# Node features for the messages kept as fp32 rows, spread by four fp32 matmuls in place of twelve bf16

## The reference, cut to what matters

```python
h = jnp.maximum(_layernorm(x, axis=-1), 0.0)
e = shifted_softplus(edge_attr_128 @ W1 + b1) @ W2 + b2      # per edge
x = x + jax.ops.segment_sum(h[dst] * e, src, num_segments=n)  # sender = dst, receiver = src
# second layer: a two-step relational graph convolution over gathered rows of h @ W[r]
```

## Time and profile before

| what | value |
|---|---|
| median of 3 runs | 7132.72 us (7132.13 to 7136.48) |
| profiled execution, its own time | 7149.41 us |
| its span | 7147.6 us |
| `prepare` | 0 to 154 us |
| `filter_layer` | 155 to 2712 us |
| `make_table` and `convolve` twice | 2712 us to the end |

### The profile page before, as it was taken

One profiled execution on the slowest core, in us unless ns is written; L12 is line 12 of the kernel. 1 busy time (PEld: TensorE's weight loads), 2 busy tenths in 40 slices (PEclk: granted clock), 3 DMA queues, 4 the chain that ended last, 5 costly groups with the idle time before them and its releaser, 6 DMA issues. The chain is left out here.

```text
span 7147.6 us, 113836 instructions
## 1 busy us (share of the span) xinstructions
PE 4359.0 (61%) x28573; PEld 3531.3 (49%) x28573; DVE 3819.8 (53%) x11981; ACT 2911.5 (41%) x7788; POOL 5383.4 (75%) x5304
## 2 busy tenths in 40 slices
PE   2888888888888887645555555555444444444444
PEld 1666666667777773444444444444333333333333
DVE  8888888868777877645555555555211111111111
ACT  2666666654444446523333333333222222222222
POOL 6777777778888885577777777777677777777777
PEclk6999999999999998756666666666555555555555
DMA  3766666589998988634444443333222222222222
GB/s 107 188 183 182 181 181 162 149 173 190 188 189 186 192 166 273 209 89 104 106 106 106 105 105 105 106 105 103 67 55 56 56 56 56 56 56 56 56 56 54
DMA packets 688258, 879.21 MB, mean 123 GB/s; under 512 B 132110, under 2 KB 512426, under 8 KB 687277
## 3 DMA queue, kind: packets, MB, share of 16 engines
q1 hardware_dynamic: 446088, 530.23, 26.9%
q0 software_dynamic: 238864, 340.26, 21.9%
q10 hardware_dynamic: 2634, 1.21, 0.1%
HBM read 615.41 MB, written 255.76 MB: 122 GB/s over the span
## 5 line engine op out<-in xcount | busy, mean ns | idle before, releaser
L1907 POOL DMA_INDIRECT got<-table_dram,cidx x3322 | 3154.0, 949 | 1057.3 <-issue 996.9
L1956 PE MATMUL bank<-got,share 128*128 128x128 f32 x6656 | 1632.7, 422 | 1856.0 <-DMA got<-table_dram,cidx 1855.5
L1956 PEld LDWEIGHTS bank<-got,share 128*128 128x128 f32 x6656 | 1400.6, 311 | 2010.3 <-DMA got<-table_dram,cidx 2009.7
L1536 POOL DMA_INDIRECT msg_dram<-total,idx x1008 | 986.7, 979 | 335.3 <-issue 281.1
L2010 ACT ACTIVATE share<-cto_node,etcol 128x128 f32<-128x128 bf16 x3328 | 1071.1, 393 | 354.0 <-DVE cto_node L2101 318.4
L1551 POOL DMA_INDIRECT acc_dram<-total,idx x653 | 1035.7, 1586 | 206.5 <-issue 194.6
L2000 ACT ACTIVATE cidx<-srccol 128x4 int32<-128x4 f32 x832 | 169.5, 205 | 2395.2 <-PE bank L1956 2381.6
L303 DVE SCALAR_TENSOR_TENSOR xs<-bank,mask_hi,xs 128x128 f32 x416 | 146.2, 351 | 1690.0 <-PE bank L1956 1690.0
L1129 PEld LDWEIGHTS bank<-w,soft 128*128 128x128 f32 x3328 | 446.1, 195 | 56.7 <-issue 41.5
L1129 PE MATMUL bank<-w,soft 128*128 128x128 f32 x3328 | 447.1, 278 | 0.0
L1120 PE MATMUL bank<-edges_t,w 128*128 128x512 f32 x832 | 428.9, 597 | 2.4 <-DVE soft L1360 2.4
(11 more groups left out here) (262 smaller groups left out, 7877.8 us busy)
## 6 DMA issues: line engine op xcount, KB each, us to landing
edges<-in_edge_attr SPq DMA_DIRECT2D x415, 256.0 KB
unit<-msg_dram SPq DMA_DIRECT2D x616, 129.0 KB
clow<-rows_dram SPq DMA_DIRECT2D x416, 128.0 KB
got<-table_dram,cidx POOLq DMA_INDIRECT x3322
table_dram<-made SPq DMA_DIRECT2D x98, 512.0 KB, 5.0
table_dram<-umade SPq DMA_DIRECT2D x98, 512.0 KB, 3.0
low<-rows_dram SPq DMA_DIRECT2D x164, 256.0 KB
win<-split_dram SPq DMA_DIRECT2D x416, 96.0 KB
```

The lines of the kernel that those rows point to most:

```text
L1536: pool.indirect_dma_start(g.msg_dram[:, :], bass.IndirectOffsetOnAxis(ap=idx[k][:, j:j + 1], axis=0), total[k][:, j, :], None).then_inc(s_ ...
L1907: pool.indirect_dma_start(got[k][:, j, :], None, g.table_dram[which][:, :], bass.IndirectOffsetOnAxis(ap=idx[k][:, j:j + 1], axis=0)).then ...
L1956: ins = nc.tensor.matmul(window[k], share[k][:, j, :], got[ka][:, j, :], start=j == 0, stop=j == TG - 1)
```

## The change

- `split_dram` (three bf16 parts, 768 bytes a row) becomes `feat_dram` (fp32, 512 bytes a row). Stores and window loads shrink from 96 KB to 64 KB for 128 rows.
- The splitting is gone: in `prepare` 22 casts on ACT and 22 subtractions on DVE, in the filter stage 44 of each. SP's stores wait for ACT alone.
- `h` in `prepare` has 6 buffers, and ACT waits for the store of the chunk six before.
- `to_edge` is fp32 in the order (part, edge), and DVE's comparison that makes it reads `low` with a step of 4 elements.
- `spread` runs one fp32 matmul for each of the four parts, not three bf16 ones.

Of the diff, in this order: DVE's list in `prepare`, SP's store, ACT's chunks, two tiles of the filter stage, PE's `spread`, DVE's `edge_hot`, DVE's plain steps.

```diff
-            split_chunks(0, 2)
             moments(1)
-            split_chunks(2, 3)
             variance(1)
-            split_chunks(3, 4)
             constants()
...
             def store(c):
-                k = c % NSP
-                sp.wait_ge(s_part3, c + 1)
-                sp.dma_start(g.split_dram[c * CB * P:(c + 1) * CB * P, :].rearrange("(b p) f -> p b f", p=P),
-                             split[k][:, :, :, :].rearrange("p b k f -> p b (k f)")).then_inc(s_split_out[k], 16)
+                k = c % NH
+                sp.wait_ge(s_h, c * CB + CB)
+                sp.dma_start(g.feat_dram[c * CB * P:(c + 1) * CB * P, :].rearrange("(b p) f -> p b f", p=P),
+                             h[k][:, :, :]).then_inc(s_h_out[k], 16)
...
-            def split_chunk(c):
+            def feature_chunk(c):
-                need(act, s_rest1, c - NH + 1)
+                need(act, s_h_out[c % NH], c // NH * 16)
                 for i in range(c * CB, c * CB + CB):
                     nc.scalar.activation(h[c % NH][:, i - c * CB, :], g.xs[:, i, :], ACT.Relu,
                                          bias=g.shift[:, i:i + 1], scale=g.rstd[:, i:i + 1]).then_inc(s_h, 1)
-                act.wait_ge(s_h, c * CB + CB)
-                need(act, s_split_out[c % NSP], c // NSP * 16)
-                nc.scalar.activation(split[c % NSP][:, :, 0, :], h[c % NH][:, :, :], ACT.Copy).then_inc(s_part1, 1)
-                if c >= LAG:
-                    second_part(c - LAG)
...
-        win = [sb(f"win{k}", [P, 3 * F], BF16) for k in range(NE)]
+        win = [sb(f"win{k}", [P, F]) for k in range(NE)]
-        to_edge = [sb(f"to_edge{k}", [P, P, TG], BF16) for k in range(2)]
+        to_edge = [sb(f"to_edge{k}", [P, TG, P]) for k in range(2)]
...
                     for j in range(TG):
-                        for part in range(3):
-                            ins = nc.tensor.matmul(bank[:, j * F:(j + 1) * F], to_edge[k][:, :, j],
-                                                   win[s.slot(NE, 2)][:, part * F:(part + 1) * F],
-                                                   start=windows.own and part == 0, stop=part == 2 or not windows.own,
-                                                   skip_group_check=not windows.own)
+                        ins = nc.tensor.matmul(bank[:, j * F:(j + 1) * F], to_edge[k][:, j, :], win[s.slot(NE, 2)][:, :],
+                                               start=windows.own, stop=True, skip_group_check=not windows.own)
...
-                v.tensor_scalar(to_edge[k][:, :, :].rearrange("p a b -> p (a b)"), low[s.slot(NE, 2)][:, 0, :],
+                v.tensor_scalar(to_edge[k][:, :, :], low[s.slot(NE, 2)][:, 0, :].rearrange("q (p j) -> q j p", j=TG),
                                 g.want[:, bass.ds(s.at(2), 1)], None, ALU.is_equal).then_inc(s_hot, 1)
...
-                    if s.slot(CHUNK_STEPS, 0) == 1:
-                        chunk_remainder(s.use(CHUNK_STEPS, 0))
-                    if s.slot(CHUNK_STEPS, 0) == 3:
-                        chunk_third(s.use(CHUNK_STEPS, 0))
```

More of the change, by code:

```diff
@@ L326, in prepare @@
     NCH, NEARLY = g.NCH, g.NEARLY
-    NSP = 4
-    NH = 4
-    NR = 3
-    LAG = 2
+    NH = 6
     PART = NCH // 3
@@ L403, in prepare @@
         h = [sb(f"h{k}", [P, CB, F]) for k in range(NH)]
-        rest = [sb(f"rest{k}", [P, CB, F]) for k in range(NR)]
-        split = [sb(f"split{k}", [P, CB, 3, F], BF16) for k in range(NSP)]
         s_binned = sem("p_binned")
@@ L429, in prepare @@
         s_h = sem("p_h")
-        s_part1 = sem("p_part1")
-        s_rest1 = sem("p_rest1")
-        s_part2 = sem("p_part2")
-        s_part3 = sem("p_part3")
-        s_split_out = [sem(f"p_split_out{k}") for k in range(NSP)]
+        s_h_out = [sem(f"p_h_out{k}") for k in range(NH)]
         x_rest = N - (NBLK - 1) * P
@@ L476, in _ @@
             sp.wait_ge(s_rows, 12 * 16)
-            for k in range(NSP):
-                sp.wait_ge(s_split_out[k], 16 * len(range(k, NEARLY, NSP)))
+            for k in range(NH):
+                sp.wait_ge(s_h_out[k], 16 * len(range(k, NEARLY, NH)))
         @block.gpsimd
@@ L564, in _ @@
                     act.wait_ge(s_norm, 4)
-                split_chunk(c)
+                feature_chunk(c)
                 if c == PART - 3:
                     deviation(1)
-            for c in range(NEARLY - LAG, NEARLY):
-                second_part(c)
             columns(2)
@@ L1015, in load_window @@
                 first = sp.value_load(g.base[0:1, bass.ds(s.at(2), 1)], min_val=0, max_val=g.NROWS)
-                sp.dma_start(win[k][:, :], g.split_dram[bass.ds(first, P), :]).then_inc(s_win[k], 16)
+                sp.dma_start(win[k][:, :], g.feat_dram[bass.ds(first, P), :]).then_inc(s_win[k], 16)
             def clear(chunk, j):
@@ L1249, in copy_factor, with chunk @@
                 nc.scalar.activation(factor[s.slot(2, 2)][:, :], bank_e[:, :], ACT.Copy).then_inc(s_ec, 1)
-            def chunk_first(m):
+            def chunk(m):
                 for b in range(CB):
@@ L1321, in other_program @@
             def other_program():
-                chunk_first(0)
-                chunk_second(0)
+                chunk(0)
                 with act.Fori(1, g.NLATE) as m:
-                    chunk_first(m)
-                    chunk_second(m)
+                    chunk(m)
                 adding(Windows(g, False), 0, PEEL)
@@ L1514, in own_program @@
                 adding(Windows(g, True), NA, 16)
-            def other_program():
-                chunk_remainder(0)
-                chunk_third(0)
-                with dve.Fori(1, g.NLATE) as m:
-                    chunk_remainder(m)
-                    chunk_third(m)
-                adding(Windows(g, False), 0, PEEL)
-            if_own(dve, g, own_program, other_program)
+            if_own(dve, g, own_program, lambda: adding(Windows(g, False), 0, PEEL))
         @block.gpsimd
```

72 lines of the change are left out of this document (12 added, 60 removed).

## The result

| kernel | median | range, runs |
|---|---|---|
| before | 7135.67 us | 7129.54 to 7137.83, 8 |
| changed | 7153.89 us | 7149.21 to 7158.30, 8 |

The changed kernel is slower: ratio 1.0027, 95% interval 1.0017 to 1.0036, or 18.2 us. The forecast was 7120.5 us, 12.2 us faster than the 7132.72 known then. The profiled execution of the changed kernel takes 7153.8 us.

A forecast was written before the change was run, and what follows sets the result against it. POOL's transfers were taken to bound the filter stage and DVE's list prepare. Prepare -13.9, first filter group -0.3 and POOL's holding +2 gave -12.2 us, from 7132.7 to 7120.5 us; range 7108 to 7135 us for 8 in 10.

The forecast's parts named there:

- Prepare: Stage before the filter stage: without DVE's 22 subtractions it ends 13.9 us earlier, between 11.1 and 14.8.
- rival 4: In prepare, POOL gets no relief and stays the bound: 7123.3 us; 55% together with the forecast itself.
- gap ahead of the second third's moments: Sign in DVE's list in prepare: none expected; a gap there would be the nodes' load.
- PE's spread: Filter stage, PE: 0.22 us longer a group with fp32 products, hidden under POOL's time, 0 us.
- to_edge's length: Filter stage, DVE: the fp32 comparison takes 0.49 us, +0.13, hidden by 0.8 us to spare, 0 us.
- What POOL itself feels: Filter stage: POOL's transfers lengthen when they start inside to_edge, +2 us in sum, between -12 and +22.
- The price: Filter stage: each POOL transfer started inside to_edge takes 0.10 us longer, read from one held transfer.
- The count: Filter stage: POOL starts falling into to_edge go from 103 to 138 over plain and adding groups.
- The missing subtractions: Filter stage, late chunks: DVE's 44 subtractions fall away, which had caught 19 POOL starts, -1.9 us.
- Rival 2: Filter stage: POOL is held for all that is left of to_edge, +13 us, 7131.5 us in all; 20%.
- Rival 3: Filter stage: POOL and DVE fall into step, a start meeting to_edge in every group, 7208 us; 8%.

The follow-up runs named there:

- e1b: Kernel before with only to_edge made fp32, PE's products still bf16, at the upper clock: 7170.74 us against 7137.21, ratio 1.0047.
- e5: Changed kernel with 22 fp32 subtractions put back into DVE's list in prepare, low clock: 8335.05 us beside 8549.64 for the kernel before.
- e6: Changed kernel with to_edge back in bf16 and twelve bf16 products on the window's upper halves, low clock: 8530.73 us against 8549.64, ratio 0.9980.

## Why the prediction was wrong

- **Prepare: right.** Forecast -13.9 us, measured -12.3 at DVE's end (141.87 against 154.19) and -13.0 at the first transfer. POOL ended at 137.9 us, forecast 138.6, so rival 4 didn't come. DVE had no gap ahead of the second third's moments.
- **PE's spread: right.** 1.06 us in 8 records, hidden at the upper clock.
- **to_edge's length: right** (0.48 at best and 0.503 us on average, forecast 0.49), and hidden as length: POOL never waited longer than its 0.3 us.
- **"What POOL itself feels", +2 us: the step that failed.** It measured +29.3 us, over its own upper bound of +22. Three things in it were wrong.
  - The price. I took 0.10 us a start from the earlier trace rows and read it as a weak hold, because `to_edge` had 0.22 us to run. It was a full hold from the mark on, 0.12 us into the transfer: 0.22 - 0.12 = 0.10. That was the very same number under a rule that I didn't look for, and one row can't tell the two. By the rule, a longer `to_edge` raises the price of a hit, from 81 to 192 ns in the plain groups (2.8 us over 34, 14.6 over 76).
  - The count. I took every start inside `to_edge` for a hit, 72 and 31 before and 96 and 42 now. Held were 34 and 9 before and 76 and 32 now. The first 0.22 us of `to_edge` hold nobody, so the longer form doubled the part that does.
  - The others. I counted `to_edge` alone. By count `to_edge` cost 11.8 + 3.1 = 14.9 us more. `to_node`, which the change doesn't touch, cost 8.8 us more in the plain groups, where it held the successor of a transfer held by `to_edge` 65 times of 76; it was 1 of 34 before, when most of these transfers missed it by a few hundredths of a us. `unit_hot` cost 5.7 us more in the adding groups. The missing subtractions gave back 2.8 us, forecast 1.9. This sum is 26.6 us; `same<-low` and the one-hots add 2.5.
- **The rivals.** Rival 2 (held for all of `to_edge`, 20%) had the mechanism of a hit, but its +13 us left out the other instructions and counted the starts as I did. Rival 3 (falling into step, 8%) had the other half in a milder form, a third of the groups and not all. Each alone gave a wrong time. The Trainium skill, SBUF — State Buffer, section "Who interferes with whom", says of DVE's two-port modes that whoever issues first has the shared pair of ports for the whole instruction, and that the other is blocked. Taken at its word it gave +13 and was nearer than my row. The trace agrees with it once the wait is counted from 0.13 us after the start, for transfers whose mark comes 0.22 us or more into `to_edge`; it doesn't show which mode DVE was in.
- **Still open.** Why transfers met `unit_hot` 123 times after 96, though its place in DVE's order stands. It went with the fp32 form in e1b too (119); over all traces it is 89 to 102 times with a bf16 `to_edge` by DVE and 118 to 126 with an fp32 one in a single piece, and 117 and 110 with short pieces. Why the first 0.15 to 0.22 us of an instruction hold nobody is not shown either, only that it is so. The swaps' worth in time by themselves at the upper clock was not reached; only the combination was.

## What to carry to other kernels

Where POOL's indirect transfers are the bound, the DVE instructions that run beside them are part of the bound: ask of each how long it is (a hit waits to its end, and here its first 0.15 to 0.22 us hit nobody), whether all its inputs lie in SBUF, and what stands one transfer period behind its end. A longer instruction with the same work can cost more than its length times its hits, and cutting it into short pieces can pay though DVE gets busier, as it did for `to_edge` and `same<-low`, and not shown for `to_node`. One row of a held transfer doesn't give a price; plot the excess against what was left of the other instruction over some tens of rows before a step rests on it.

## What the runs showed of the hardware

- The hold is on tensor operations with two SBUF inputs, too. `to_node`, a comparison of two bf16 SBUF operands, held transfers for 0.16 us on average, in the same way as `to_edge`, a comparison with a scalar; instructions with a PSUM operand didn't. The Trainium skill, SBUF — State Buffer, section "Who interferes with whom", says that a DVE instruction with two SBUF inputs contends with a GpSimd instruction that reads SBUF. The trace agrees, as these transfers read `idx` and `total` there.
- An fp32 result makes the comparison with a scalar 0.48 us where the bf16 one takes 0.34 (best cases), whether it reads in steps or straight.
- The same change can have either sign. In the run with a granted clock of 0.83 in the plain groups, where POOL waited for the product, the changed kernel was 2.6% faster than before; at 1.00, with POOL never waiting, it was 0.27% slower. In the pair measured together (e5 and e6), four fp32 products in place of twelve bf16 went with 223 us less waiting. Their records are not shorter, neither at the upper clock (1.06 against 0.83 us a group) nor in that pair (1.27 against 1.00 us). Why the waiting fell is open, and that the clock is its cause is not shown; no run took it apart.
